# Score products of both self-attentions on four 64 by 64 tiles of the array, and what goes with it

## The reference, cut to what matters

```python
# layer 0: 16 heads of 32;  layer 1: 16 heads of 64, rotary and causal
h = layernorm(x)
q, k, v = (split_heads(h @ W + b) for W, b in ((Wq, bq), (Wk, bk), (Wv, bv)))
# layer 1 only: q, k = rope(q), rope(k)
p = softmax(q @ k.T * scale)        # per sequence and head, 64 by 64
x = x + merge_heads(p @ v) @ Wo + bias
```

## Time and profile before

| what | us |
|---|---|
| median of 3 runs | 1078.42 (1078.15 to 1079.48) |
| the profiled execution, its own time | 1079.72 |
| its span, first to last instruction | 1077.8 |
| layer 0 self-attention, four turns | about 165 to 279 in the span |
| layer 1 self-attention, four turns | about 747 to 1004 |

### The profile page before, as it was taken

The page is one execution under the profiler, slowest core; times in us unless marked ns, Lnnn a source line. Parts: engine busy times, 40 slices in busy tenths (PEclk is TensorE's granted clock), DMA queues, the critical chain, the costliest instruction groups (busy, mean ns, idle before and its releaser), DMA issues.

```text
span 1077.8 us, 16886 instructions
## 1 busy us (share of the span) xinstructions
PE 1056.4 (98%) x6186; PEld 663.5 (62%) x6202; DVE 638.7 (59%) x1118; ACT 347.2 (32%) x984; POOL 207.9 (19%) x201
## 2 busy tenths in 40 slices
PE   9999999999999999999999999999999999999898
PEld 5556658888544444444444465557789697887443
DVE  3254346877856622356762164457776938569777
ACT  1322256566521000121111032236442514225534
POOL 0011101333222222000001611131414123150002
PEclk9999999999999999999999999999999999999999
DMA  9996902001025590015546469974000000031105
GB/s 337 378 330 223 352 1 79 2 0 40 20 96 172 152 39 1 0 54 186 165 117 231 151 220 369 367 255 157 1 2 1 2 1 0 0 113 60 60 1 78
DMA packets 68610, 129.60 MB, mean 120 GB/s; under 512 B 9424, under 2 KB 13520, under 8 KB 68176
## 3 DMA queue, kind: packets, MB, share of 16 engines
q1 hardware_dynamic: 67696, 127.38, 36.6%
q0 software_dynamic: 864, 1.57, 1.2%
HBM read 120.92 MB, written 8.01 MB: 120 GB/s over the span
## 4 chain that ended last, share of the span: by engine, by line
PE 65%; issue 11%; DVE 10%; POOL 6%; ACT 3%; SPq 3%; DMA 1%; DVEq 0%; POOLq 0%; ACTq 0%
PE bank L2164 26%; PE bank L2191 5%; PE bank L482 5%; PE bank L450 4%; PE bank L404 3%; PE bank L2403 3%; PE bank L980 2%; PE bank L1701 2%; PE bank L527 2%; PE bank L516 2%; DVE s_e L1924 2%; ACT s_e L1071 2%; PE bank L502 2%; DMA x_proj<-in_x_pw_dram 1%; PE bank L2448 1%
## 5 line engine op out<-in xcount | busy, mean ns | idle before, releaser
L2209 ACT ACTIVATE f_act<-bank,f_sgn 128x512 f32<-128x512 f32 x64 | 44.0, 687 | 261.8 <-PE bank L2164 257.3
L2164 PE MATMUL bank<-f_a_lo,f_w 128*128 128x512 f16 x512 | 115.7, 379 | 0.0
L2164 PE MATMUL bank<-f_a_hi,f_w 128*128 128x512 f16 x512 | 115.7, 379 | 0.0
L2164 PEld LDWEIGHTS bank<-f_a_lo,f_w 128*128 x512 | 50.1, 98 | 60.4
L2164 PEld LDWEIGHTS bank<-f_a_hi,f_w 128*128 x512 | 50.1, 98 | 60.2
L2264 DVE CAST f_b_hi<-f_act 128x512 f16<-128x512 f32 x32 | 26.7, 834 | 95.7 <-ACT f_act L2209 95.6
L1924 DVE TENSOR_TENSOR s_e<-s_pair,s_tables 128x512 f32<-128x512 f32 x64 | 41.4, 688 | 33.1 <-POOL s_kT L2001 21.5
L450 PE MATMUL bank<-x_cT,x_qT 128*64 128x512 f32 x256 | 58.5, 598 | 0.0
L482 PE MATMUL bank<-x_cN,x_eT 128*64 128x512 f32 x256 | 56.9, 596 | 0.0
L1909 DVE TENSOR_TENSOR s_k_diag<-s_kT,s_spread 128x512 f32<-128x512 f32 x64 | 47.1, 787 | 0.1
L1804 ACT ACTIVATE s_e<-bank,s_nmax 128x64 f32<-128x64 f32 x128 | 38.1, 337 | 24.9 <-DVE s_nmax L1868 24.7
(11 more groups left out here) (348 smaller groups left out, 2323.6 us busy)
## 6 DMA issues: line engine op xcount, KB each, us to landing
x_cT<-in_ctx_cols_dram SPq DMA_DIRECT2D x32, 1024.0 KB, 8.6
x_cN<-in_ctx_rows_dram SPq DMA_DIRECT2D x32, 1024.0 KB, 11.1
f_upper_bits<-in_f_w_dram SPq DMA_DIRECT2D x20, 256.0 KB, 4.2
f_row<-in_f_wg_dram SPq DMA_DIRECT2D x11, 256.0 KB, 3.4
f_long_row<-in_f_wd_dram SPq DMA_DIRECT2D x4, 704.0 KB, 5.7
f_row<-in_f_wu_dram SPq DMA_DIRECT2D x11, 256.0 KB, 2.8
f_part<-in_f_wgT_dram SPq DMA_DIRECT2D x8, 352.0 KB, 3.5
f_part<-in_f_wuT_dram SPq DMA_DIRECT2D x8, 352.0 KB, 3.3
```

The costliest lines, as they stand in the source:

```text
L2164: mm = pe.matmul(h_bank[s][:, :], weights(2 * i + s, k), part[:, k, cols], start=(n == 0 and k == 0), stop=(n == 1 and k == k_chunks - 1))
L2209: act.activation(act32[s][:, :], h_bank[s][:, :], ACT.Relu, scale=sgn[:, layer % 2:layer % 2 + 1]).then_inc(h_read, 1)
```

## The change

In both self-attentions a score product of 128 features by 64 tokens is split by rows into two: features 0 to 63 (two heads) and features 64 to 127 (two heads). Each of the four (half n, sequence b) uses its own 64 by 64 tile of the array, with a moving operand of 128 columns in place of 256; half n goes to bank `S_BANK[s][n]`. The diagonals so hold two blocks in place of four. The order of heads in the banks changes, and with it the indices of maxima, sums and values. Both maxima of an s now wait for all four groups. A `nop` that cannot be merged stands between the waits and the first product of a group (layer 1) or of `scores(0, ...)` (layer 0). In layer 0 the banks of s = 0 and s = 1 are exchanged and the first half's values are copied by DVE, between the normalised x and maximum (1, 0), and no longer by ACT. In layer 1 all four groups of s = 0 stand ahead of `open_scores(1)` and the second value projection; the three diagonal buffers become six in the same space; the maximum (0, 0) moves behind the diagonals (1, 0) and (1, 1).

```diff
-        k_diag = sb("k_diag", [P, KC, 4, 4, SEQ])
+        k_diag = sb("k_diag", [P, KC, 4, 2, SEQ])
...
-        S_BANK = [[0, 1], [2, 3]]
+        S_BANK = [[2, 3], [0, 1]]
...
-        X_BANK = [0, 1]
+        X_BANK = [2, 3]
...
-            def scores(s, n):
-                for g in (2 * n, 2 * n + 1):
-                    cols = slice((g % 2) * 4 * SEQ, (g % 2 + 1) * 4 * SEQ)
+            def scores(s, groups):
+                if s == 0:
+                    pe.nop(nofuse=True)
+                for g in groups:
+                    cols = slice(g * 2 * SEQ, (g + 1) * 2 * SEQ)
                     for b in range(2):
                         tokens = slice(s * P + b * SEQ, s * P + (b + 1) * SEQ)
-                        mm = pe.matmul(bank[S_BANK[s][n]][SEQ * b:SEQ * (b + 1), cols], qT[:, g, tokens],
-                                       k_diag[:, g, 2 * s + b, :, :].rearrange("p j n -> p (j n)"), start=True, stop=True, skip_group_check=True)
+                        for n in range(2):
+                            rows = slice(n * SEQ, (n + 1) * SEQ)
+                            mm = pe.matmul(bank[S_BANK[s][n]][SEQ * b:SEQ * (b + 1), cols], qT[rows, g, tokens],
+                                           k_diag[rows, g, 2 * s + b, :, :].rearrange("p j n -> p (j n)"), start=True, stop=True, skip_group_check=True)
                 mm.then_inc(s_done, 1)
...
-                    for j in range(4):
+                    for j in range(2):
                         ins = act.activation(k_diag[:, c, :, j, :],
...
-                act.wait_ge(v_done, 2 * i + 1)
-                if first:
-                    act.wait_ge(set_ok, 1)
-                for b in range(2):
-                    for a in range(2):
-                        v_pairs = bank[V_BANK[0]][SEQ * b:SEQ * (b + 1), :].rearrange("p (m a e) -> p m a e", a=2, e=HD)
-                        ins = act.copy(v_diag[0][SEQ * a:SEQ * (a + 1), b, :, a, :], v_pairs[:, :, a, :])
-                ins.then_inc(v0_ok, 1)
                 exponentials(i, 1, 0)
...
             def negative_maxima(i, s, n):
-                dve.wait_ge(s_done, 4 * i + 2 * s + n + 1)
+                dve.wait_ge(s_done, 4 * i + 2 * s + 2)
...
-                    for j in range(4):
+                    for j in range(2):
                         ins = dve.tensor_scalar(k_diag[:, c, :, j, :],
...
                     normalise_x(2 * i + 2, i + 1)
+                copy_values(0, 2 * i + 1, v0_ok, first)
                 negative_maxima(i, 1, 0)
...
-            self.k_diag = [first(f"k_diag{n}", [P, AB, 2, 4 * SEQ]) for n in range(2)]
+            diagonals = [first(f"k_diag{n}", [P, 2, AB, 2, 2 * SEQ]) for n in range(2)]
...
-            Front.reserve_around(sb, "over_front", self.k_diag, [P, AB, 2, 4 * SEQ])
+            Front.reserve_around(sb, "over_front", diagonals, [P, 2, AB, 2, 2 * SEQ])
+            self.k_diag = [two[:, n, :, :, :] for two in diagonals for n in range(2)]
...
                     pe.wait_ge(kd_ok, 8 * i + 4 * s + g + 1)
                     pe.wait_ge(rope_ok, 8 * i + GROUPS + g + 1)
+                    pe.nop(nofuse=True)
                     for a in range(AB):
                         for b in range(2):
                             tokens = slice(s * P + b * SEQ, s * P + (b + 1) * SEQ)
-                            mm = pe.matmul(at[SEQ * b:SEQ * (b + 1), cols], qT[:, g, a, tokens], k_diag[(4 * s + g) % KD][:, a, b, :],
-                                           start=False, stop=(a == AB - 1), skip_group_check=True)
+                            for n in range(2):
+                                rows = slice(n * SEQ, (n + 1) * SEQ)
+                                mm = pe.matmul(bank[S_BANK[s][n]][SEQ * b:SEQ * (b + 1), cols], qT[rows, g, a, tokens],
+                                               k_diag[(4 * s + g) % KD][rows, a, b, :], start=False, stop=(a == AB - 1), skip_group_check=True)
...
                 open_scores(0)
-                scores(i, 0, (0, 1))
+                scores(i, 0, range(GROUPS))
                 pe.wait_ge(q_read, GROUPS * (i + 1))
                 open_scores(1)
                 project_values(0, (1,))
-                scores(i, 0, (2, 3))
                 scores(i, 1, (0, 1))
...
             def negative_maxima(i, s, n):
-                dve.wait_ge(s_done, 8 * i + 4 * s + 2 * n + 2)
+                dve.wait_ge(s_done, 8 * i + 4 * s + GROUPS)
...
                         ins = dve.tensor_tensor(
-                            k_diag[n % KD][:, a, :, :].rearrange("p b (j n) -> p b j n", j=4),
+                            k_diag[n % KD][:, a, :, :].rearrange("p b (j n) -> p b j n", j=2),
...
                 dve.wait_ge(rope_ok, 8 * i + 8)
-                negative_maxima(i, 0, 0)
                 spread_keys(1, 0)
                 spread_keys(1, 1)
+                negative_maxima(i, 0, 0)
                 negative_maxima(i, 0, 1)
```

More of the change, by code:

```diff
@@ L1012, in attend @@
                     for j in range(4):
-                        m = 4 * n + j
+                        m = 2 * j + n
                         for b in range(2):
@@ L1028, in turn @@
                 pe.wait_ge(q_read, 2 * i + 1)
-                scores(0, 0)
+                scores(0, (0, 1))
                 pe.wait_ge(k1_ok, i + 1)
                 pe.wait_ge(q_read, 2 * i + 2)
-                scores(0, 1)
+                scores(0, (2, 3))
                 if not first:
@@ L1037, in turn @@
                 project_values(0)
-                scores(1, 0)
-                scores(1, 1)
+                scores(1, (0, 1))
+                scores(1, (2, 3))
                 project_values(1)
@@ L1069, in exponentials @@
                 for j in range(8):
-                    h = 8 * n + j
+                    at, h = 8 * n + j, 4 * (j // 2) + 2 * n + j % 2
                     ins = act.activation(e_sb[s][n][:, j * SEQ:(j + 1) * SEQ], bank[S_BANK[s][n]][:, j * SEQ:(j + 1) * SEQ], ACT.Exp,
-                                         bias=nmax[s][:, h:h + 1], accum_out=total[s][:, h:h + 1])
+                                         bias=nmax[s][:, at:at + 1], accum_out=total[s][:, h:h + 1])
                 ins.then_inc(e_ok, 1)
@@ L1140, in negative_maxima, with copy_values @@
             def negative_maxima(i, s, n):
-                dve.wait_ge(s_done, 4 * i + 2 * s + n + 1)
+                dve.wait_ge(s_done, 4 * i + 2 * s + 2)
                 dve.tensor_reduce(nmax[s][:, 8 * n:8 * n + 8], bank[S_BANK[s][n]][:, :].rearrange("p (j k) -> p j k", j=8),
                                   AX_X, ALU.max, negate=True).then_inc(max_ok, 1)
+            def copy_values(s, done, copied, first):
+                dve.wait_ge(v_done, done)
+                if first:
+                    dve.wait_ge(set_ok, s + 1)
+                for b in range(2):
+                    for a in range(2):
+                        v_pairs = bank[V_BANK[s]][SEQ * b:SEQ * (b + 1), :].rearrange("p (m a e) -> p m a e", a=2, e=HD)
+                        ins = dve.tensor_copy(v_diag[s][SEQ * a:SEQ * (a + 1), b, :, a, :], v_pairs[:, :, a, :])
+                ins.then_inc(copied, 1)
             def copy_weights(i, s, n):
@@ L1204, in turn @@
                 copy_weights(i, 0, 1)
-                dve.wait_ge(v_done, 2 * i + 2)
-                if first:
-                    dve.wait_ge(set_ok, 2)
-                for b in range(2):
-                    for a in range(2):
-                        v_pairs = bank[V_BANK[1]][SEQ * b:SEQ * (b + 1), :].rearrange("p (m a e) -> p m a e", a=2, e=HD)
-                        ins = dve.tensor_copy(v_diag[1][SEQ * a:SEQ * (a + 1), b, :, a, :], v_pairs[:, :, a, :])
-                ins.then_inc(v1_ok, 1)
+                copy_values(1, 2 * i + 2, v1_ok, first)
                 copy_weights(i, 1, 0)
@@ L2707, in layout @@
     io["past"] = c(np.broadcast_to(np.where(past, 0.0, -1e30).astype(bf16)[:, None, :], (P, 8, SEQ)))
-    io["spread"] = (p[:, None] // 32 == np.arange(4)[None, :]).astype(np.float32)
+    io["spread"] = (p[:, None] % 64 // 32 == np.arange(4)[None, :]).astype(np.float32)
     half = 32
```

7 lines of the change are left out of this document (3 added, 4 removed).

## The result

The median fell from 1078.86 us (4 runs, 1078.15 to 1079.48) to 1062.51 us (4 runs, 1062.41 to 1063.30). The ratio is 0.985, 95% interval 0.9835 to 0.9866. The forecast was 1059.0 with a range of 1055 to 1070: faster, as said, by 16.4 us where 19.4 were forecast. That is inside the range, and 0.5 us above the band of 1055 to 1062 that had a chance of 0.55.

A forecast was written before the change was run, and what follows sets the result against it. PE was taken to bound the kernel, as long as the chain over DVE and ACT follows. Layer 0 -8.8, layer 1 -11.6 and nops +1 sum to -19.4 us, from the median 1078.4 to 1059.0; range 1055 to 1070.

The forecast's parts named there:

- Four tiles at once: Score products in both layers: all four tiles overlap, 0.032 us taken per record, between 0.027 and 0.034.
- rival 1: Score products: only two tiles run at once, 0.059 us a record; about 1070 us; chance 0.15.
- rival 2: Two tiles at once and POOL's layer 1 rounds do not shorten; 1077 us, about no change; chance 0.07.
- rival 3: Score products: the four tiles take turns, 0.109 us a record, slower at about 1111 us; chance 0.06.
- rival 4: All as forecast, but tiles reach 0.045 us a record; 6 us less gained, 1065 us; chance 0.13.
- Layer 0's first burst: First 32 score records of a layer 0 turn: 1.05 us where 16 took 2.02.
- the 0.2 of waits: Layer 0's first and last turns: PE waits less for ACT, 0.2 us beside 1.8 of products, 2.0 each.
- Layer 0's middle turns: Two middle turns of layer 0: ACT ends about 2.5 us earlier, PE follows by about 2.4 us each.
- ACT's copies: Layer 0: value copies leave ACT (-1.57 us) and join DVE (1.72 us); ACT loses 0.4 to the maximum.
- POOL's rounds: Layer 1: three rotary rounds beside DVE's halved diagonals lose 0.5 us less each; the chain ends 1.6 us earlier.
- PE idle ahead of group 3: Layer 1, s = 0: PE waits 1.4 us for DVE's diagonal of group 3, formerly covered by the value projection.
- Nops: 40 nops ahead of score products: 1 us taken for all, between 0 and 3.

The follow-up runs named there:

- experiment 1: Changed kernel with layer 0's first-half value copies given back to ACT: 1067.18 us.
- experiment 2: Kernel before the change, with only layer 0's first-half value copies moved to DVE, ahead of maximum (1, 0): 1076.09 us.
- experiment 8: Changed kernel with each layer 1 diagonal written twice by DVE, once into a buffer nobody reads: 1079.55 us.
- experiment 3: Changed kernel with each of its 40 nops doubled: 1062.55 us.
- experiment 6: Changed kernel with three diagonal buffers of the new size in layer 1 instead of six: 1062.98 us.
- fourth experiment: Changed kernel with score products reordered so that each tile's products in a burst are issued together: 1062.20 us.
- experiment 10: Changed kernel with layer 0's sign transposes moved between the two halves of the first score burst: 1063.82 us.
- experiment 9: Changed kernel with layer 1's diagonal of s = 0, group 3 made ahead of the last round's products: 1060.05 us.
- experiment 11: Changed kernel with both layer 1's early group 3 diagonal and layer 0's sign transposes between the score halves: 1061.71 us.
- experiment 12: Changed kernel with, in layer 1, the early group 3 diagonal, maximum (0, 0) ahead of diagonals (1, 0) and (1, 1), second masks ahead of group 3: 1057.79 us.
- experiment 5: Changed kernel with PE's old layer 1 order, groups 2 and 3 of s = 0 behind the second value projection: 1067.87 us.

## Why the prediction was right, and where it was not

- **Four tiles at once: right.** 0.027 us a record, the quarter of 0.109 and not the 0.032 taken. With its start a burst of 32 costs 1.03 us (1.05 in the sum) and a group of 16 by itself 0.60 (0.53 in the sum). Rivals 1 to 4 fall with it. The Trainium skill (TensorEngine Tiling (Array Packing), Key Properties) has the drain on a change of mode only. The step from the last four projection records to the first score, 0.57 us from 229.73 to 230.30, is as long as before the change (203.79 to 204.36 in the second turn): the trace agrees in that the smaller tiles add nothing there. Its speed-up of 3.07 for four row tiles (TensorE: Matmul & The Clock Gate, Measured speedup vs the span model) is not what these tiles do: 0.109 / 0.027 = 4.0.
- **Layer 0's first burst: the term that was mis-sized.** The prediction took 1.05 us and wrote the 0.14 between 2.02 and 1.88 off to surroundings, next to tile changes. It was a wait for ACT. The weight loads of the kernel before, third turn of layer 0, have it:

```profile
233.52 0.63 PEld L996 LDWEIGHTS bank<-s_k_diag,s_qT 128*64 128x64 f32 x8
234.52 0.63 PEld L996 LDWEIGHTS bank<-s_k_diag,s_qT 128*64 128x64 f32 x8 [0.37 <-ACT s_qT L1090]
```

  ACT's copy of the last queries ends 0.95 us after the first score starts, in both kernels. The first half of the old burst (0.94) all but covered it; the new one (0.45) doesn't, and the burst takes 1.09 + 0.60 = 1.69. It saves 0.33 us in place of 0.97 (0.45 of 2.10 in the first turn). In the first and the last turn this and the 0.2 of waits, which did not come, are the whole miss: 0.45 + 0.84 = 1.29 for a measured 1.27, 0.33 + 0.84 = 1.17 for 1.10.
- **Layer 0's middle turns: 2.27 for 2.4, near, with two errors that cancel.** The scores were done 0.64 us later than reckoned, and so the first exponential came 0.8 us earlier in the turn and not 1.4; but ACT lost nothing to maximum (1, 0) where 0.4 had been set. It ends 0.8 + 1.6 = 2.4 us earlier, 2.5 were forecast. Of the 0.8, 0.33 are the burst. The other half microsecond is DVE's half as many diagonals: before, DVE was held by its subtraction until 236.2, though the scores were done at 235.5; now it waits for them.
- **ACT's copies: right in kind** (experiments 1 and 2). That the two parts need each other, 3.2 of 6.9 us, was in the argument (PE follows only as far as it has less to do) but not in a number.
- **POOL's rounds: right.** 3.14 us for 3.67, 0.5 a round as forecast. The eighth experiment shows how much hangs on DVE's diagonals, some 2.5 us a turn without the clock's part.
- **PE idle ahead of group 3: right, 1.7 for 1.4** (1.3 to 2.2 over the four turns). Group 3 starts 3.22 us after the first score, 2.96 were reckoned. DVE was on time: the second operation of the diagonal starts at 827.74 and lasts 0.42, so it is over 2.98 after the first score. The 0.24 from there to PE's first product (828.40) stood at nothing in the sum. The first exponential comes at 5.07 for 4.9; the end of the weighted sum 12.46 for 12.11. So 2.41 us for 2.75, and the later wait for `v_diag` shrank from 0.38 to 0.15 as said. In all 2.6 a turn for 2.9: no other step, the 0.26 us that group 3 was late carried through.
- **Nops: 0, not 1 us** (experiment 3). Six buffers: nothing, right (experiment 6).
- **The sum.** -6.9 and -10.3 make the 17.2 us between the two spans. The forecast's 19.4 less 1.9 (layer 0), less 1.3 (layer 1), plus 1 for the nops is 17.2. In the medians it is 16.4, since the profiled execution of the kernel before took 1079.72, 0.9 above its median, and that of the changed kernel 0.1 under its own. Inside layer 0 errors cancel in part, and the 1 us for nops, which did not come, makes up for a third of the 3.2 missed in the layers: that the total is so near is partly luck.

## What was not expected: the clock

The prediction did not look for this. The kernel before has a granted clock of 1.00 in all executions but for two at 0.999. In the changed one three of four show 0.998. The profile of the fourth experiment caught it. Its windows in the last turn of layer 1, PE idle ahead of group 3, then what follows:

```profile
950.00:952.40 2.40, 1.11 (x19) 0.83 (x20) 2.39 (x7) 0.00 (x0) 0.22 (x1) 1.00 1.03 432
952.40:956.00 3.60, 3.60 (x11) 2.80 (x10) 2.71 (x7) 2.76 (x19) 0.00 (x0) 0.53 0.98 358
```

and its timeline of PE there:

```profile
951.29 0.69 PE L1659 MATMUL bank<-s_k_diag,s_qT 64*64 64x128 f32 x16 [2.07 <-DVE s_k_diag L1911]
...
952.16 2.02 PE L1638 MATMUL bank<-s_wv_hi,x_xT_hi 128*128 128x512 f32 x4
```

After 2.07 us of idle time the clock fell from 2.4 to 1.2 GHz (0.53 in the window) for some 3.5 us, and the value products took twice as long. The last stretch of layer 1 was 38.6 us where the profiled execution of the changed kernel has 37.2. That execution had an idle time of 2.20 us in the same place and no fall:

```profile
952.60:956.00 3.40, 3.39 (x29) 2.62 (x30) 3.37 (x9) 1.44 (x10) 0.00 (x0) 1.00 1.00 372
```

So it happens in some executions and not in others: with 2.07 to 2.54 us idle in the last turn, 12 of 27 executions have 0.998 (three of four of the changed kernel, none of four in experiment 1). In experiment 6 the two executions at 1.00 took 1061.42 and 1061.75 us, the three at 0.998 took 1062.98 to 1063.60. In the profiles that caught it (experiments 4, 6 and 10) layer 1 is 1.2 to 1.7 us longer than in the changed kernel's. What it costs the changed kernel's own median can't be read: its execution at 1.00 took 1062.41 us, the three at 0.998 took 1062.47 to 1063.30, and the stretch ahead of layer 0 varies by more than that.

With less idle time it was not seen: the fifteen executions of experiments 9, 11 and 12 all have 1.00, and their idle time ahead of group 3 is 0.4 to 1.0 us in the second turn, 1.3 to 1.5 in the last. With more of it, it came in every execution: experiment 5 (0.994 to 0.997; idle 2.45 us in each turn, and in the profile a fall behind two of the four), experiment 8 (0.989 to 0.994; idle 3.3 to 3.9 us, a fall behind each). The last turn also has heavy transfers (DMA share 1.03 and 0.98 above), but they are not needed for it: in the second turn of experiment 8 the share is 0.00. So an idle stretch that a reorder opens can cost one to two microseconds more behind it. That it is the idle time, and not something else that these kernels share, was not tried by itself.

## What to carry to other kernels

Narrow products that can be split by rows onto four 64 by 64 tiles ran at four times the rate of full-array records with as many columns (0.027 for 0.109 us), in both orders tried, and a burst of scores took 1.03 us in place of 1.88; the nops between them cost nothing that shows. What then counts is what the long burst had covered, so read the weight loads' waits as well as PE's before halving it, for a wait of 0.1 us can stand for one of 0.4. Where two engines are within a microsecond of each other in a turn, shortening one alone gives little: cost the parts of such a change as a pair. And read the granted clock behind a new idle stretch of PE: here 2.1 to 2.5 us of it came with a fall in some executions, and what closed it was to reorder what its producer does first.
